# Two gated attention and feed-forward layers on one core: scores from one stacked contraction, queries copied by DMA into blocks, stages of a unit spread over more slots

## What is computed

```
attn = softmax(einsum('bqhd,bkhd->bhqk', q, k) * scale (+ distance_bias))
out  = einsum('bhqk,bkhd->bqhd', attn, v) @ w_o.T
wq   = clip(round(w / s), -1, 1) * s            # s = mean |w|
xq   = clip(round(x * 127 / max|x|), -128, 127) * max|x| / 127
```

## Time and profile before

| | us |
|---|---|
| median of three executions | 470.06 (464.96 to 476.62) |
| the profiled execution | 465.11 |
| its span, first to last instruction | 463.4 |

### The profile page before, as it was taken

How to read it: one execution, slowest core, us unless ns; L and a number is a source line. 1 busy time by engine, 2 the same in 40 slices (tenths; PEclk the granted TensorE clock), 3 DMA queues, 4 the chain that set the end, 5 groups by cost and what they waited for, 6 DMA issues and landing times.

```text
span 463.4 us, 9962 instructions
## 1 busy us (share of the span) xinstructions
PE 390.0 (84%) x3756; PEld 308.1 (66%) x3756; DVE 345.0 (74%) x765; ACT 269.5 (58%) x487; POOL 282.0 (61%) x413
## 2 busy tenths in 40 slices
PE   4689789987997985875858799889998989999990
PEld 3557466655664753553546688778898879988880
DVE  7886566898888666688878756887875775877665
ACT  1547257864863458988863477445566655555630
POOL 6896845755865830387776743766777447444553
PEclk9999899998997696889879999999999999999996
DMA  8960000000000000000031000000000000110001
GB/s 255 287 173 1 0 2 1 0 4 0 2 2 1 2 1 0 0 1 1 2 120 62 2 1 1 3 1 1 1 1 1 3 2 1 37 33 24 25 24 45
DMA packets 13065, 13.07 MB, mean 28 GB/s; under 512 B 3468, under 2 KB 12429, under 8 KB 12941
## 3 DMA queue, kind: packets, MB, share of 16 engines
q1 hardware_dynamic: 13018, 12.44, 9.1%
HBM read 10.34 MB, written 2.10 MB: 27 GB/s over the span
## 4 chain that ended last, share of the span: by engine, by line
PE 60%; DVE 24%; issue 6%; ACT 5%; POOL 4%; DMA 1%; POOLq 0%; DVEq 0%; ACTq 0%
PE psD L1163 6%; PE psR L1241 5%; PE psS L1437 5%; PE psD L1420 5%; PE psD L1159 4%; PE psR L1420 4%; PE psD L1165 4%; PE psD L1164 4%; DVE ham L954 3%; PE psBE L1437 3%; DVE mx L897 3%; PE psBE L1187 3%; DVE m L922 2%; PE psD L1161 2%; PE psD L1162 2%
## 5 line engine op out<-in xcount | busy, mean ns | idle before, releaser
L397 POOL TENSOR_TENSOR pp_lo<-p,pp_hi 124x512 f16<-124x512 f32 x80 | 98.1, 1242 | 38.3 <-ACT pp_hi L572 38.1
L309 POOL TENSOR_TENSOR lns<-lns,mhalf 128x2 f32<-128x2 f32 x40 | 28.7, 719 | 118.9 <-DVE lns L698 112.8
L897 DVE TENSOR_REDUCE mx<-psBE 128x6 f32<-128x462 f32 (+1 forms) x96 | 54.1, 580 | 39.4 <-PE psBE L1187 39.4
L566 ACT ACTIVATE p<-psD 124x512 f32<-124x512 f32 x80 | 47.6, 596 | 34.3 <-PE psD L1165 33.5
L1163 PE MATMUL psD<-q_hi,kt_hi 128*124 128x256 f16 x160 | 48.8, 305 | 0.0
L572 ACT ACTIVATE pp_hi<-p 124x512 f16<-124x512 f32 x80 | 48.5, 624 | 0.0
L1165 PE MATMUL psD<-q_hi,kt_lo 128*124 128x256 f16 x160 | 44.7, 279 | 0.0
L1164 PE MATMUL psD<-q_lo,kt_hi 128*124 128x256 f16 x160 | 44.6, 279 | 0.0
L472 ACT ACTIVATE xT_hi<-psS 128x512 f16<-128x512 f32 x23 | 13.6, 592 | 33.6 <-PE psS L1078 33.5
L990 DVE TENSOR_TENSOR pp_lo<-space,pp_hi 128x512 f16<-128x512 f32 x32 | 24.3, 777 | 11.8 <-ACT space L646 11.6
L1187 PE MATMUL psBE<-kt_hi,q_hi 128*128 128x308 f16 (+2 forms) x128 | 31.7, 297 | 1.5 <-DVE kt_hi L733 1.5
(11 more groups left out here) (227 smaller groups left out, 1359.6 us busy)
## 6 DMA issues: line engine op xcount, KB each, us to landing
xs<-in_x SPq DMA_DIRECT2D x8, 256.0 KB, 6.0
tw_raw<-in_tw SPq DMA_DIRECT2D x2, 1024.0 KB, 11.8
space<-in_ew SPq DMA_DIRECT2D x2, 1024.0 KB, 6.2
out<-space SPq DMA_DIRECT2D x8, 256.0 KB, 2.1
space<-in_distN SPq DMA_DIRECT2D x1, 616.0 KB
space<-in_distT SPq DMA_DIRECT2D x1, 616.0 KB
wspace<-in_wk SPq DMA_DIRECT2D x2, 256.0 KB, 5.1
wspace<-in_wv SPq DMA_DIRECT2D x2, 256.0 KB, 5.3
```

Of the source, the lines that this page charges most:

```text
L397: nc.gpsimd.tensor_tensor(pl[:, u % 2, 2 * r:2 * r + 2, :], p32[:, n % 4, :, :], ph[:, u % 2, 2 * r:2 * r + 2, :], ALU.subtract).then_inc( ...
L566: a_(p32[:, n % 4, :, :], psD[n % 2][0:KR, :].rearrange("p (t r) -> p t r", t=2), ACT.Exp, scale=1.0 / SSC).then_inc(a["exp"], 1)
L897: v.tensor_reduce(mx[:, s % 2, j, 6 * k:6 * k + hn], psBE[:, n % 2, 0:hn * KEYS].rearrange("p (h k) -> p h k", h=hn), AX.X, ALU.max).then_ ...
```

## The change

**Scores.** Each head pair g of a half has a block of q rows, `qb`: 32 rows of q_hi, 32 of q_lo, 32 of q_hi again, 2 rows of shifts, 98 in all. `ktb` stacks the same heads' keys: high, high, low, and -1024 for the shifts. One matmul gives what four gave for the heads of that pair; a tile of 124 keys touches one or two pairs, so a unit has 16 such matmuls. In layer 1 `qb` has 26 more rows, of the bias' low part, and one matmul per tile over `bb` adds the rest of the bias: 26 matmuls a unit.

**Copies.** [...] `qb` has three buffers. [...]

**Shifts.** `mx` is transposed as float32 (`shifts_transposed`), scaled and offset on ScalarE (`shifts`).

**Banks.** Maxima keep `psBE`; values have `psV`, queries `psQ`; the four kinds of transposes and the projection share `psX`.

**Order.** Score pairs 0 to 2 of unit s-1 stand in rounds 2 to 4, pairs 3 and 4 of unit s-2 in rounds 0 and 1 of a slot. Shifts and the next unit's queries stand at the slot's end. Input transposes stand in round 0, output transposes in 2, the projection in 4. The division is one for the whole unit, at the start of the next slot. The normalised rows of s-4 are made on ScalarE (two passes with scale and bias) from factors of GpSimd. Ternary weights are rounded by two comparisons on VectorE without ScalarE, four pieces in slots 3 to 6, four in slots 8 and 9. `keep_busy` is gone.

```diff
 
-        psD2, psBE, psR, psS = psum("psD", 2), psum("psBE", 2), psum("psR", 2), psum("psS", 2)
+        psD2, psBE, psA = psum("psD", 2), psum("psBE", 2), psum("psA", 4)
         psD = [psD2[:, i, :] for i in range(2)]
-        psQ, psG = psR[:, 0, :], psS[:, 0, :]
-        psT = [psS[:, 1, :], psR[:, 1, :]]
+        psQ, psV, psX = psA[:, 0, :], psA[:, 1:3, :], psA[:, 3, :]
+        psG = psA[:, 2, :]
...
+            def key_blocks(l):
+
+                if l == 0:
+                    sp.wait_ge(s_const, C_KTB)
+                else:
+                    sp.wait_ge(A[0]["psc"], 5 * NU)
+                sp.wait_ge(s_kt, 4 * l + 4)
+                for g in range(GH):
+                    rows = slice(g * QB, (g + 1) * QB)
...
+                    for p in (0, 1):
+                        sp.dma_start(ktb[p * QB:(p + 1) * QB, :, g, at],
+                                     kt[rows, :, :, cols].rearrange("p c b k -> p (c b) k")).then_inc(d_ktb, 16)
+                sp.wait_ge(s_ktl, l + 1)
+                for g in range(GH):
+                    rows = slice(g * QB, (g + 1) * QB)
+                    at = slice(g * (2 * KEYS - KR), g * (2 * KEYS - KR) + 2 * KEYS)
...
+            def head_pairs(l, u, p, t):
+
+                for g in range(GH):
+                    sp.dma_start(qb[p * QB:(p + 1) * QB, u % NQ, :, g, :],
+                                 t[g * QB:(g + 1) * QB, u % 2, :, :]).then_inc(d_q[u % NQ], 16)
+
+            def query_blocks(l, u):
+
+                a, i = A[l], u % NQ
+                sp.wait_ge(a["qhi"], u + 1)
+                if l == 1 and u == 0:
+                    sp.wait_ge(A[0]["psc"], 5 * NU)
+                ge(sp, a["psc"], 5 * (u - NQ + 1))
+                for p in (0, 2):
+                    head_pairs(l, u, p, q[0])
+                if l == 1:
+                    v = bT[1][BLO:KEYS, u * UR:(u + 1) * UR]
+                    sp.dma_start(qb[QL:QL + KEYS - BLO, i, :, :, :].rearrange("p c g r -> p (c g) r"),
+                                 v.unsqueeze(1).to_broadcast([KEYS - BLO, GH * DK, UR])).then_inc(d_q[i], 16)
+                sp.wait_ge(a["qlo"], u + 1)
+                head_pairs(l, u, 1, q[1])
+
+            def shift_rows(l, u):
+
+                a, i = A[l], u % NQ
+                sp.wait_ge(a["mTc"], u + 1)
+                for r in (0, 1):
+                    sp.dma_start(qb[QM + r:QM + r + 1, i, :, :, :].rearrange("p c g r -> p (c g) r"),
+                                 mT[r:H:2, u % 2, :]).then_inc(d_q[i], 16)
+
+            for u in (0, 1):
+                load_x(u)
             sp.dma_start(ctxT[:, :, :], io["ctxT"].rearrange("(c p) k -> p c k", p=128)).then_inc(d_ctx, 16)
...
+            key_blocks(0)
+            query_blocks(0, 0)
+            sp.dma_start(tw1_raw[:, :, :], io["tw1"].rearrange("(c p) n -> p c n", p=128)).then_inc(d_tw1, 16)
+            for u in (6, 7):
+                load_x(u)
+            shift_rows(0, 0)
+            query_blocks(0, 1)
+            sp.dma_start(tw2_raw[:, :, :], io["tw2"].rearrange("(c p) n -> p c n", p=128)).then_inc(d_tw2, 16)
+            shift_rows(0, 1)
+            query_blocks(0, 2)
+            load_w(1, "kv")
+            shift_rows(0, 2)
+            query_blocks(0, 3)
...
+            def factors_act(n, scale, done):
+
+                g = factors(n, scale)
+                link(nc.gpsimd.tensor_tensor(g[:, 6, :], g[:, 5, :], mv[:, n % 4, :, 0], ALU.mult))
+                nc.gpsimd.tensor_scalar(g[:, 7, :], g[:, 6, :], -1.0, None, ALU.mult).then_inc(done, 1)
+
...
-
-            for s in range(NU + 3):
+                if not 0 <= u < NU:
+                    return
+                n = 5 * u + r
+                pool.wait_ge(a["phi"], n + 1)
+                ge(pool, a["ppv"], 2 * (u - 1))
+                nc.gpsimd.tensor_tensor(pl[:, u % 2, 2 * r:2 * r + 2, :], p32[:, n % 4, :, :],
...
+                if 0 <= s - 4 < NU:
+                    factors_act((1 + 2 * l) * NU + s - 4, (1.0, SX)[l], A[l]["fac"])
+                for u, r in ((s - 2, 3), (s - 2, 4), (s - 1, 0), (s - 1, 1)):
+                    plo(l, u, r)
+
...
-                if s in (3, 4) and r in (1, 2, 4, 5):
-                    i = {1: 0, 2: 1, 4: 2, 5: 3}[r]
-                    if s == 3 and i == 0:
-                        act.wait_ge(s_ws, 1)
-                    k = s - 3
-                    raw = tw_raw[:, k, i * 512:(i + 1) * 512]
-                    a_(raw, raw, ACT.Identity, scale=wrs[:, k:k + 1], bias=epsc[:, 3:4]).then_inc(s_tr, 1)
...
+            def queries_hi(l, u):
+
+                a = A[l]
+                act.wait_ge(a["pq"], u + 1)
+                ge(act, a["psc"], 5 * (u - 2) + 1)
+                if l == 0:
+                    i = a_(q[0][:, u % 2, :, :].rearrange("p c r -> p (c r)"), psQ[:, :], ACT.Copy)
+                else:
+                    for c in range(DK):
...
+            def normalised(l, u):
+
+                a = A[l]
...
+                elif u == 0:
+                    act.wait_ge(s_tw, 8)
+                n = (1 + 2 * l) * NU + u
+                out = xn[:, u % 2, :, :] if l == 0 else xnk[:, 2 * u:2 * u + 2, :]
+                for j in (0, 1):
+                    i = a_(out[:, j, :], xs[:, 2 * u + j, :], ACT.Identity, scale=lns[:, n % 4, 5, j:j + 1],
+                           bias=lns[:, n % 4, 7, j:j + 1])
+                i.then_inc(a["app" if l == 0 else "xn"], 1)
...
+            def shifts(l, u):
+
+                a = A[l]
+                act.wait_ge(a["pmT"], u + 1)
+                ge(act, a["psc"], 5 * (u - 1))
+                a_(mT[:, u % 2, :], psBE[0:H, 0, 0:UR], ACT.Identity, scale=1.0 / SM,
+                   bias=epsc[0:H, 6:7]).then_inc(a["mTc"], 1)
...
-                link(v.tensor_scalar(raw, raw, MAGIC, 1.0, ALU.subtract, ALU.min))
-                v.tensor_scalar(w, raw, -1.0, None, ALU.max).then_inc(s_tw, 1)
+                dve.wait_ge(s_abs, 2)
+                link(v.tensor_scalar(w, raw, wrs[:, 1, k:k + 1], None, ALU.is_lt))
+                v.scalar_tensor_tensor(w, raw, wrs[:, 0, k:k + 1], w, ALU.is_gt, ALU.subtract).then_inc(s_tw, 1)
 
...
+            def divide(l, u):
+
+                a = A[l]
+                dve.wait_ge(a["ppv"], 2 * u + 2)
+                ge(dve, a["poT"], u - 1)
+                banks = psV[:, :, 0:H * VW].rearrange("p j (h c) -> p j h c", c=VW)
+                link(v.reciprocal(rec[:, :, :], banks[:, :, :, HD]))
+                v.tensor_tensor(o32[:, u % 2, :, :].rearrange("p j (h d) -> p j h d", h=H), banks[:, :, :, 0:HD],
+                                rec[:, :, :].unsqueeze(3).to_broadcast([128, 2, H, HD]), ALU.mult).then_inc(a["norm"], 1)
...
-            def keep_busy(n, bank):
-
-                for _ in range(n):
-                    mm(bank[:, UR:2 * UR], ones16[:, 0:128], ones16[:, :], start=True, stop=True)
...
             def scores(l, u, r):
 
                 a, b = A[l], u // UPB
...
                 if r == 0:
-                    pe.wait_ge(a["qhi"], u + 1)
-                    pe.wait_ge(a["qlo"], u + 1)
-                    pe.wait_ge(a["mTc"], u + 1)
+                    pe.wait_ge(d_q[u % NQ], QN[l] * (u // NQ + 1) + l * QN[0] * len(range(u % NQ, NU, NQ)))
                     if u == 0:
...
+                            pe.wait_ge(d_bb, 16)
+                        pe.wait_ge(d_ktb, 12 * 16 * (l + 1))
+                        pe.wait_ge(s_bm, 2)
                 n = 5 * u + r
                 ge(pe, a["exp"], n - 1)
...
                 for k in (0, 1):
                     hf, t = divmod(2 * r + k, TPH)
                     o = psD[n % 2][0:KR, k * UR:(k + 1) * UR]
-                    c = slice(t * KR, (t + 1) * KR)
-                    if l == 0:
-                        mm(o, mind[:, hf, c], mT[M0:, u % 2, :], start=(k == 0), stop=False)
-                    else:
-                        mm(o, selm[:, hf, c], bmT[:, u * UR:(u + 1) * UR], start=(k == 0), stop=False)
-                        mm(o, sel[:, c], bT[1][:, u * UR:(u + 1) * UR], start=False, stop=False)
-                    mm(o, kt[0][:, hf, b, c], q[0][:, u % 2, hf, :], start=False, stop=False)
-                    mm(o, kt[0][:, hf, b, c], q[1][:, u % 2, hf, :], start=False, stop=False)
-                    i = mm(o, kt[1][:, hf, b, c], q[0][:, u % 2, hf, :], start=False, stop=(k == 1))
+                    first = k == 0
+                    if l == 1:
+                        mm(o, selb[:, t * KR:(t + 1) * KR], bb[:, u * UR:(u + 1) * UR], start=first, stop=False)
+                        first = False
+                    for g in range(max(t - 1, 0), min(t + 1, GH)):
+                        i = mm(o, ktb[0:rows, hf * B + b, g, (t - g) * KR:(t - g + 1) * KR], qb[0:rows, u % NQ, hf, g, :],
+                               start=first, stop=(k == 1 and g == min(t + 1, GH) - 1))
+                        first = False
                 i.then_inc(a["psc"], 1)
...
-                ge(pe, a["oTh"], min(s - 2, NU))
```

(35 more changed lines are left out.)

559 lines of the change are left out of this document (277 added, 282 removed).

## The result

| | median us | executions | ratio to before |
|---|---|---|---|
| before | 468.64 | 464.96 to 476.62 | |
| changed | 484.31 | 483.36 to 485.03 | 1.039, 95% interval 1.034 to 1.044 |

Slower by 3.9%, where I had forecast 453 us, faster by 3.6%. The time lies outside my range of 432 to 475. Executions more than 1.5% slower than the fastest of their kernel are counted as a slower state, and the ratios leave them out (in e_all2 two of six, in some rounds one to three of the kernel before); the medians don't. The profiled execution has a span of 482.2 us against 463.4: the stages differ by 18.8 us where I expected -11.5.

The account below looks back on a forecast made before the run. It took TensorE to bound both layers' steady slots, ScalarE and VectorE the ternary stretch. Terms -8 - 9 + 3 - 1 + 0 - 3 - 2.5 + 1 + 8 = -11.5 on 465.1 us gave 453 us, range 432 to 475.

Parts of the forecast that it names:

- just enough: 0, and +4 if it is not: Start: slot 1's old end at 52.5 us covers the wait for the second ternary weight; 0, otherwise +4 us.
- slot 2's start later than 58 us: Sign in the new profile: if the slot after the tables begins later than 58 us, the forecast is wrong at the start.
- the other slots together -2.5: Layer 1 outside its four steady slots and slot 9: the other slots together get 2.5 us shorter.
- Slot 9: +3: End of layer 0: slot 9 takes over score tiles, low halves and ternary rounds from earlier slots; +3 us.
- slot 9 +1: End of layer 1: slot 9 gets 1 us longer.
- Steady slots: Slots 3 to 6: layer 0 falls to 52 from 60.2 us, -8; layer 1 to 13.4 from 14.1 a slot, -3.
- the chain through psX: Shared bank of transposes and projection: ten hops between engines, at 0.1 us more each, cost 1 us a slot.
- +8: TensorE's clock: thinner slots run partly at 1.2 GHz, in layer 0, layer 1 and the start; +8 us in all.
- a clock below 0.75 over 69 to 120 us: Sign in layer 0's steady stretch that the low clock rival holds.
- The one that ends slower: Rival: shift rows land late in every slot, costing what exceeds 3.1 us; 486 us at a 5.3 us landing; chance 0.08.
- The change of order gives nothing: Rival: hops between engines on the chain through psX add 1 us a slot; 469 us; chance 0.10.
- low clock: Rival: clock stays low through both attention layers; 483 us at worst, 470 if half the slots are slow; chance 0.12.

Follow-up runs that it names:

- e_all2: The changed kernel with the edits of e_twoq and e_keys2 together; 460.0 us, ratio 0.983 to the kernel before.
- e_start: The changed kernel with the two ternary weights issued between layer 0's high and low key copies on SyncE; 474.1 us, ratio 1.017.
- e_twoq: e_start with unit 0's eight q_hi copies issued from ScalarE's queue, q_lo copies ahead of the low key copies; 474.4 us, ratio 1.015.
- e_keys: The changed kernel with all four keys_high of layer 1 made in ternary slot 4; 480.8 us, ratio 1.032.
- e_keys2: The changed kernel with layer 1's keys spread over four earlier slots, and expert matmuls ahead of output transposes in layer 1's drain; 478.3 us, ratio 1.023.
- e_psx: The changed kernel with ScalarE's xT_hi moved to the head of its round, in each slot from 5 on; 481.6 us, ratio 1.030.
- e_drain: The changed kernel with the next stage's matmuls ahead of the output transposes in slots 9 and 10 of both layers; 488.6 us, ratio 1.051.
- e_dorder: The changed kernel with VectorE's ternary reductions behind the residual in slots 9 to 12 of layer 0; 491.7 us, ratio 1.054.
- e_dlite: The changed kernel with the last two ternary rounding pieces in slot 10 of layer 0 instead of slot 9; 486.8 us, ratio 1.042.
- e_clock: The changed kernel with filler matmuls in slots 4 to 7 of layer 0; 484.4 us, ratio 1.037.
- e_loads: The changed kernel with both ternary weights and the inputs of units 6 and 7 issued ahead of the key copies; 474.8 us, ratio 1.022.

## Why the prediction was wrong

**Start: the step that failed first.** I summed "one per 0.49 us" from HBM loads to 13 us and called the cover "just enough: 0, and +4 if it is not". It was +10.9 with slot 2. Four things were mis-sized. An SBUF copy's issue takes 0.65 us. The chain was also blocked for 3.5 us by GpSimd's low keys. The shift rows landed 3.9 us later behind loads than without them (e_start), and I had put the first score at 42 where it came at 46.66. And the second ternary weight, which I had issued "at 42" and waited for "until about 48", was issued at 50.05 and waited for until 55.66; I priced its lateness against slot 1's old end, without asking what stands behind ScalarE's wait: exponentials, hence GpSimd's low halves, hence the values. e_start (-10.7 at q_hi of slot 3) shows it by removal, and e_twoq's edit takes off a further 3.4 from the first q_hi to that of slot 3 in all five profiles that have it. The profile's check that I had named, slot 2's start later than 58 us, was met: 60.4. "The fillers ... removing them saves nothing" left out what they did for the clock, 0.93 before and 0.54 now in 34 to 60 us; its price at the start stays open.
The Trainium skill (DMA: Bandwidth & Descriptors, Issuing engines are not separate DMA queues) says that starting DMAs from several engines saves only the time to initiate them, "usually small relative to the DMA itself". What it calls saved is what e_twoq moved to a second queue. It was not small here: one issue takes 0.65 us of the queue where a key copy lands 2.0 us after its issue, and 26 of them in a row are 17 us. The DMA view's row (count, KB each, us to landing):
```profile
ktb<-kt_hi SPq DMA_DIRECT2D x16, 38.5 KB, 2.0
```

**Layer 1's first slots.** My term was "the other slots together -2.5". I had not put a price on the second filling of the pipeline: 27 issues (12 for keys, 13 for queries and bias, 2 for shift rows) after VectorE's last keys. The term was missing, not mis-sized; slot 1 grew by 8.0 us. e_keys and e_keys2 took 5.8 and 4.7 of them back. e_all2 took 8.9, and the 4.2 beyond e_keys2 came with full clock in that slot.

**The drains.** "Slot 9: +3" and "slot 9 +1" were +7.5 (with the ternary stretch) and +9.4. My reading is that a stage that comes a slot later is free in a steady slot and is added once in a drain. For layer 1 a part of it was shown: e_keys2 and e_psx each give 4.2 us back, and with the first TensorE's wait for xT_lo in these slots falls from 7.7 to 2.4 us. The other 5 to 6 us stay unexplained. For layer 0 nothing was: three edits (e_drain, e_dorder, e_dlite) moved the wait, none shortened the stage, and two made it longer. What sets it, beyond VectorE's and ScalarE's common order there, stays open.

**Steady slots: faster as forecast, the size short.** Layer 0's four slots gave -5.8 for -8, layer 1's -1.8 for -3. TensorE was relieved, and the slot fell to a chain like the one I had laid out, with one link placed wrong: I wrote that the sixth maximum, "behind quantise, is done by then". In layer 0 it was among what ended the slot. With it moved and fillers in, a slot is 12.6 us; the layout had 12.4, and 13 with the copies that I had added. The shared bank was not the last chain in layer 0: with out_T 0.9 us earlier (e_psx) the slots kept their length. My layout had the projection done at 7.5 and GpSimd's low halves at 8.4, so it fits that; "the chain through psX" in my rivals doesn't. The move of the maximum without the fillers was not tried.

**The clock.** I charged +8 and spread it over the slots. The dips in layer 0 are real: the granted clock was 0.51 in 102.8 to 106.3 and 0.50 in 113.1 to 116.5, behind stops of TensorE. But in these four slots the profiles from 0.82 to 1.00 lie 2 to 4 us apart, and e_clock's 1.5 us didn't reach the end. The sign that I had set, a clock below 0.75 over 69 to 120 us, was not met: 0.84. Where the clock did weigh is layer 1's slot 1, 4.2 us in one slot between 0.69 (e_keys2) and 1.00 (e_all2), where my term had a tenth of 3.5 us for a slot; what it costs at the start was not measured. So the term was too large for the steady slots and too small for this one, and its sum in the changed kernel stays open. I also read the row before wrongly: a mean of 0.97 is full clock for 94% of the stretch, not 97%, if the rest is at half. By the rule of the Trainium skill (TensorE: Matmul & The Clock Gate, HAM oscillation) as I applied it, the thinner slots would all be slow; the trace has 0.91 over layer 0's four slots and 0.97 over layer 1's, so it bears that out in places only. The page draws it from a kernel that waits longer ahead of each burst of matmuls than the burst takes; here TensorE is busy 39.3 of 54.5 us, so I had stretched the rule. This term hid part of the other errors: without it I was 38 us short, not 30.

**The rivals.** The one that ends slower had the right resource, the shift rows, and the wrong place: it charged them per slot, where TensorE's five waits for them in the whole kernel are 23.4 us and the two long ones 19.4 of these, once per layer. A landing over its 3.1 us did come, behind the loads of the start: the second shift row was issued at 40.7, and the first score followed at 46.66. "The change of order gives nothing" was nearer; it too had no term for the edges. All my rivals were about the slot that repeats 16 times, so the whole range missed what happens twice. I had given 0.11 to slower; by the list above it, late rows 0.08 and half of the low clock's 0.12, it should have been 0.14.

## What to carry over

When a change moves stages of a software pipeline apart or puts a copy between two engines, cost it in three places: the repeating slot, the fill and the drain; and in fill and drain follow what stands behind each new wait on its engine. Count DMA issues as serial work of the queue, at the price of the same kind of copy, look for the last producer ahead of the whole block of them, and keep large loads out of the time in which a small copy must land. When two profiles of a stage differ, compare the granted clock before crediting the edit. Clearing the edges turned this change from 3.9% slower to 2.9% faster, a part of it by full clock in layer 1's slot 1, while one move of a wait in a drain cost 7 us alone.

## What was not expected of the hardware

- A copy of 32 KB inside SBUF, 32 partitions to 32 partitions, holds its queue for 0.65 us (8 in 5.17), on SyncE as on ScalarE (8 in 5.22); a shift-row copy 0.7. Loads had 0.49.
- The issue of two 256 KB input loads took 6.5 us of the queue in e_loads, at 18.5 behind 26 other loads, and 1.0 us in the changed kernel, at 38.8. What filled up was not tried.
- What half clock costs depends on the slot: full instead of partly halved clock bought 1.5 of 54 us in layer 0's slots 3 to 6, and 4.2 of 19 us in layer 1's slot 1 with the same instructions (0.69 in e_keys2, 1.00 in e_all2).
- Small copies landed behind large loads issued just ahead of them: in the changed kernel, e_start and e_twoq the first score started 0.3 to 0.5 us after the last load ahead of the shift rows had landed.
